# First edge stage of a two-layer graph network: the running sum of messages closed by a TensorE matmul and copied out by ScalarE

## What is computed

```
q_i = q[dst]; k_j = k[src]; v_j = v[src]
dk = silu(edge_attr @ Wdk.T + bdk); dv = silu(edge_attr @ Wdv.T + bdv)
attn = sum(q_i * k_j * dk, axis=1)
attn = silu(attn) * cosine_cutoff(edge_weight)
msg  = v_j * dv * attn[:, None]
agg  = segment_sum(msg, dst, num_segments=6250)
```

## Time and profile before

| | us |
|---|---|
| median of 3 runs | 3669.13 (3664.78 to 3677.05) |
| profiled execution | 3659.42 |
| its span, first to last instruction | 3657.6 |
| chunk loop of `edges_0` in it, first to last addition of a total | 265.4 to 1374.1 |

### The profile page before, as it was taken

How to read it: one execution, slowest core, us unless ns; L and a number is a source line. 1 busy time by engine, 2 the same in 40 slices (tenths; PEclk the granted TensorE clock), 3 DMA queues, 4 the chain that set the end, 5 groups by cost and what they waited for, 6 DMA issues and landing times. The chain is left out here.

```text
span 3657.6 us, 111781 instructions
## 1 busy us (share of the span) xinstructions
PE 3381.2 (92%) x25829; PEld 2771.8 (76%) x25830; DVE 3185.6 (87%) x9898; ACT 2594.7 (71%) x7607; POOL 2390.0 (65%) x2549
## 2 busy tenths in 40 slices
PE   3979999999999997996999999999999999997997
PEld 2547777777777775775888888888888888886996
DVE  6768999999999995664999999999999999996775
ACT  1856777777777774543878888888888888884553
POOL 3756777777777763554666666666666666663775
PEclk8989999999999997998999999999999999998998
DMA  3979999999999984776888888888888888884663
GB/s 102 263 230 309 301 296 301 298 298 298 299 298 300 300 253 165 276 258 224 254 235 239 240 236 239 237 239 237 238 238 239 238 237 239 236 237 150 213 208 126
DMA packets 604966, 898.40 MB, mean 246 GB/s; under 512 B 208971, under 2 KB 418646, under 8 KB 604371
## 3 DMA queue, kind: packets, MB, share of 16 engines
q0 software_dynamic: 164240, 566.71, 50.5%
q1 hardware_dynamic: 440643, 330.78, 30.2%
HBM read 724.25 MB, written 175.28 MB: 246 GB/s over the span
## 5 line engine op out<-in xcount | busy, mean ns | idle before, releaser
L1595 POOL DMA_INDIRECT kv1c<-kv_table,rec x900 | 865.9, 962 | 299.0 <-issue 284.6
L916 POOL DMA_INDIRECT kv<-kv_table,rec x832 | 848.3, 1020 | 282.3 <-issue 258.2
L1700 DVE CUSTOM_DVE_ANT_0 masked_scores<-score_p,far 126x384 f32<-126x384 f32 x1200 | 595.6, 551 | 30.2 <-issue 14.1
L1640 ACT ACTIVATE wv<-kv1c,wv 128x64 f32<-128x64 f32 x2400 | 605.9, 335 | 17.7
L954 ACT ACTIVATE gates<-gates_p 128x512 f32<-128x512 f32 x832 | 448.3, 591 | 77.5 <-PE gates_p L1087 77.5
L1803 PE MATMUL sum_p<-wv,hot 128*126 128x260 f32 x1800 | 477.7, 402 | 1.4 <-ACT wv L1640 1.4
L1759 PE MATMUL qe_p<-qrel,hotT 126*128 126x256 f32 x1800 | 443.0, 382 | 22.7 <-ACT hotT L1625 18.1
L1107 PE MATMUL sum_p<-msg,hot_weighted 128*124 128x256 f32 x1664 | 416.2, 393 | 5.3 <-ACT hot_weighted L962 5.3
L1759 PEld LDWEIGHTS qe_p<-qrel,hotT 126*128 126x128 f32 x1800 | 343.7, 191 | 74.9 <-ACT hotT L1625 18.7
L1107 PEld LDWEIGHTS sum_p<-msg,hot_weighted 128*124 128x124 f32 x1664 | 295.2, 187 | 116.2 <-issue 73.9
L1803 PEld LDWEIGHTS sum_p<-wv,hot 128*126 128x126 f32 x1800 | 316.1, 189 | 76.1 <-ACT wv L1640 1.8
(11 more groups left out here) (285 smaller groups left out, 7392.0 us busy)
## 6 DMA issues: line engine op xcount, KB each, us to landing
key<-segment_keys SPq DMA_DIRECT2D x300, 192.0 KB
q_blk<-q_table SPq DMA_DIRECT2D x208, 256.5 KB
acc_table<-acc SPq DMA_DIRECT2D x300, 130.0 KB
qrel<-q_by_relation SPq DMA_DIRECT2D x300, 128.0 KB
feat<-in_edge_feat_t SPq DMA_DIRECT2D x208, 128.0 KB
agg_and_x_plus_h<-total SPq DMA_DIRECT2D x208, 128.0 KB
kv1c<-kv_table,rec POOLq DMA_INDIRECT x900
kv<-kv_table,rec POOLq DMA_INDIRECT x832
```

The costliest lines, as they stand in the source:

```text
L916: pool.indirect_dma_start(kv[it.slot(AHEAD)][:, t, :], None, c["kv0_d"], bass.IndirectOffsetOnAxis(ap=rec[k][:, t, 0:1].bitcast(I32), axis ...
L1595: pool.indirect_dma_start(kv[k][:, t, :], None, c["kv1_d"], bass.IndirectOffsetOnAxis(ap=rec[k][:, t, 0:1].bitcast(I32), axis=0)).then_inc ...
L1640: ins = act.activation(wv[k][:, t, h, 0:DK], kv[s][:, t, D + h * DK:D + (h + 1) * DK], ACT.Copy, scale=wv[k][:, t, h, DK:DK + 1])
L1700: dve.tensor_tensor_reduce(junk[k][:, h], score_p[:, :, h, :], far[it.slot(U1)][:], 1.0, FLOOR, ALU.subtract, ALU.max, top[s][:, h:h + 1]) ...
```

## The change

DVE's `add_total` goes. In its place:

- ACT gets `same_diagonal(s-2)`: it scales a 124 x 124 identity by the flag `keep`, into one of two new buffers `same`.
- PE's `sum_messages(s-3)` gets a fifth 32-bit matmul into the same accumulation: `same` (124 x 124) against the total of the item before (124 x 256). Its four first matmuls now wait for the total of two items before instead of one, and the fifth waits for `same` and for the total of the item before.
- ACT gets `total_out(s-3)`: it copies the finished sum from PSUM into the slot of total. Both new functions stand ahead of `attn_silu` in ACT's order, `total_out` first.

```diff
--- before.py
+++ after.py
@@ -812,6 +812,7 @@
         weight = [sb(f"weight{k}", [P, T0]) for k in range(2)]
         msg = [sb(f"msg{k}", [P, T0, D]) for k in range(2)]
         total = [sb(f"total{k}", [P, D]) for k in range(U)]
+        same = [sb(f"same{k}", [GROUP, GROUP]) for k in range(2)]
         iota_0 = sb("iota_0", [P, GROUP])
         gates_p = [ps(f"gates_p{t}", [P, 2 * D]) for t in range(T0)]
         qe_p = ps("qe_p", [P, T0, D])
@@ -828,6 +829,7 @@
         qe_ready, qk_ready, attn_ready = sem("qe_ready"), sem("qk_ready"), sem("attn_ready")
         attn_act_ready, weight_ready = sem("attn_act_ready"), sem("weight_ready")
         msg_ready, msg_summed, total_ready = sem("msg_ready"), sem("msg_summed"), sem("total_ready")
+        same_ready = sem("same_block_diagonal")
         stored, held, iota_ready = sem("total_stored"), sem("edge0_held"), sem("iota_0_ready")
         LOADS = 3
 
@@ -954,6 +956,18 @@
                             act.activation(gates[k][:, t, :], gates_p[t][:], ACT.Silu).then_inc(gates_ready, 1)
                     return f
 
+                def total_out(it):
+                    k, s = it.slot(2), it.slot(U)
+                    wait(act, msg_summed, it)
+                    wait(act, stored, it, U, per=16)
+                    act.copy(total[s][0:GROUP], sum_p[:, k, :]).then_inc(total_ready, 1)
+
+                def same_diagonal(it):
+                    wait(act, keep_ready, it)
+                    wait(act, msg_summed, it, 2)
+                    act.activation(same[it.slot(2)][:], c["ident"][0:GROUP, 0:GROUP], ACT.Copy,
+                                   scale=keep[it.slot(U)][:]).then_inc(same_ready, 1)
+
                 def weigh_hot(it):
                     k = it.slot(2)
                     wait(act, weight_ready, it)
@@ -963,7 +977,7 @@
                                              scale=weight[k][:, t:t + 1])
                     ins.then_inc(hot_w_ready, 1)
 
-                run_chunks(act, steps, ((1, hot_out), (0, split_lead), (2, attn_silu), (1, gates_silu(1)),
+                run_chunks(act, steps, ((1, hot_out), (0, split_lead), (3, total_out), (2, same_diagonal), (2, attn_silu), (1, gates_silu(1)),
                                         (2, weigh_hot), (0, gates_silu(0))), U)
 
             @block.vector
@@ -1027,15 +1041,6 @@
                                                        ALU.mult, ALU.add, attn[k][:, t:t + 1])
                     ins.then_inc(attn_ready, 1)
 
-                def add_total(it):
-                    k, s = it.slot(2), it.slot(U)
-                    wait(dve, keep_ready, it)
-                    wait(dve, msg_summed, it)
-                    wait(dve, stored, it, U, per=16)
-                    wait(dve, total_ready, it, 1)
-                    dve.scalar_tensor_tensor(total[s][0:GROUP], total[it.prev().slot(U)][0:GROUP], keep[s][:],
-                                             sum_p[:, k, :], ALU.mult, ALU.add).then_inc(total_ready, 1)
-
                 def weights(it):
                     k, s = it.slot(2), it.slot(U)
                     wait(dve, attn_act_ready, it)
@@ -1054,7 +1059,7 @@
                                       ALU.mult).then_inc(msg_ready, 1)
 
                 run_chunks(dve, steps, ((2, q_times_k), (2, messages), (2, scores), (0, one_hot), (0, same_block),
-                                        (0, split_rest), (2, weights), (3, add_total)), U)
+                                        (0, split_rest), (2, weights)), U)
 
             @block.tensor
             def _(pe):
@@ -1102,11 +1107,13 @@
                     k = it.slot(2)
                     wait(pe, hot_w_ready, it)
                     wait(pe, msg_ready, it)
+                    wait(pe, total_ready, it, 2)
+                    for t in range(T0):
+                        pe.matmul(sum_p[:, k, :], hot_w[k][:, t, :], msg[k][:, t, :], start=t == 0, stop=False)
+                    wait(pe, same_ready, it)
                     wait(pe, total_ready, it, 1)
-                    for t in range(T0):
-                        ins = pe.matmul(sum_p[:, k, :], hot_w[k][:, t, :], msg[k][:, t, :],
-                                        start=t == 0, stop=t == T0 - 1)
-                    ins.then_inc(msg_summed, 1)
+                    pe.matmul(sum_p[:, k, :], same[k][:], total[it.prev().slot(U)][0:GROUP], start=False,
+                              stop=True).then_inc(msg_summed, 1)
 
                 run_chunks(pe, steps, ((1, edge_gates), (3, sum_messages), (1, q_of_edges), (0, turn)), U)
```

## The result

The changed kernel took 3721.8 us (median of 4 runs, 3716.8 to 3727.8), the one before 3667.0 beside it: ratio 1.0148, 95% interval 1.0135 to 1.0161, some 55 us slower. The forecast was slower by 90 us, 3759, with a range from 3738 to 3790. The sign was right, the size wrong, and the time lies outside the range: the change costs three fifths of what I had worked out.

A forecast was written before the change was run, and what follows sets the result against it. The prediction took the first edge stage to be PE-bound by its list; +86 us in the middle and +4 in ramp and drain, on 3669.1, gave 3759 us, range 3738 to 3790.

The forecast's parts named there:

- So PE's own list fills 5.27 of the 5.29 us: First edge stage: PE's gates, sums, q and transposes, summed start to start, take 5.27 us with no wait between.
- right behind: First edge stage: DVE and the loop through `qe_p`, 5.36 us in the step read, come just after PE's list.
- eight records in 1.99 us in the drain: Drain of first edge stage: sum records with data ready take the usual 1.99 us, so the pace is PE's own.
- The fifth matmul, 0.47 us: PE's message sums: two more records of 0.235 us each, making the step 5.74 us.
- the lower end of the range: Whole kernel: 3745 us with the ramp swallowed and runs near the profiled one; 3738 with some slack on PE.
- Rival 2: PE's list contains hidden slack that the fifth matmul fills; the `qe_p` loop keeps the pace, time 3669 us; chance 0.05.
- DVE's addition gives back nothing on the path: DVE loses 97.8 us of busy time, but `q_times_k` still waits for PE's q; 0.02 us a step taken.
- ACT's wait fits into the step: ACT's `total_out` waits for the same step's sum; its loop of 5.41 to 5.63 us stays under 5.74.
- DVE waits for ACT's silu, covered by q: DVE's `weights` waits for the later silu; DVE is back at about 807.1, PE's q ends at 807.18: barely covered.
- Other stages unmoved: Outside the first edge stage: all other stages run the same code, and everything behind the loop is merely shifted.
- PE still without idle time: Sign expected in the profile after: PE shows no idle time, in steps of 5.74 us.

The follow-up runs named there:

- e8: Changed kernel without its fifth matmul, ACT's copy and diagonal behind the gates, DVE's order q_times_k, one_hot, scores, messages: ratio 0.9906, step 5.131 us.
- e3: Kernel before, with DVE's addition cut to one of its 256 columns, nothing added to PE or ACT: ratio 0.9993, step 5.283 us.
- e10: Kernel before, with only DVE's order changed to q_times_k, one_hot, scores, messages: ratio 0.9987, step 5.276 us.
- e4: Kernel before, with DVE's addition cut to one column and DVE's scores put ahead of its messages: ratio 1.0001, step 5.319 us.
- e2: Kernel before, with two more 32-bit matmuls per step in the message sums (zero tile, adds nothing): ratio 1.0370, step 6.001 us.
- e1: Kernel before, with one more 32-bit matmul per step in the message sums (zero tile), DVE's addition kept: ratio 1.0146, step 5.571 us.
- e6: Changed kernel with ACT's copy and diagonal behind the gates and DVE's order q_times_k, one_hot, scores, messages: ratio 1.0130, step 5.570 us.
- e5: Changed kernel with ACT's copy and diagonal moved behind attn_silu and the second half of the gates, ahead of weigh_hot: ratio 1.0127, step 5.571 us.
- e12: Changed kernel with total and diagonal in rounded 32-bit format, ACT's copy behind the gates, DVE's order q_times_k, one_hot, scores, messages: ratio 0.9962, step 5.253 us.
- e11: Kernel before, DVE's order q_times_k, one_hot, scores, messages; ACT copies the sum from PSUM, DVE adds it from SBUF one step later: ratio 1.0041, step 5.396 us.

## Why the prediction was wrong

- **"So PE's own list fills 5.27 of the 5.29 us"**: this is the step that failed. The list takes 5.13 us (e8). I summed distances from start to start and took the lack of idle time between records for the lack of waiting. The record of the last sum reaches past the point where the next matmul could have begun, and q's late start lay under it. What held the step was the loop through `qe_p`: shorten DVE's list and nothing happens (e3), loosen the loop and PE's idle time ahead of q goes (e8, e10). The numbers for it stood in my own text: scores end at 805.39, q starts at 805.53, in a loop that I had summed to 5.36 us and called "right behind". It was in front.
- **The evidence that I gave for it**, eight records in 1.99 us in the drain, holds for the records of the sums among themselves, and says nothing of the wait between them and q. What I needed was q's start behind the sums with the scores done: 1.64 us (e4, e8), not 1.88.
- **The row that would have told**: the earlier trace rows counts 21 steps in which q's weight load waited for DVE. The rest of the idle time there, 44.6 us in 149 steps, was under "issue", and I left it out. The two together are 0.30 us a step over all 170 steps, of which 0.06 stay when nothing is waited for (e8).
- **The fifth matmul, 0.47 us**: mis-sized by a little. The full price is 0.43 to 0.44 (e2 less e1, e6 less e8); my 0.235 a record came from 1.88 / 8, which carried part of q's wait. For a part of it being hidden I had allowed next to nothing: 0.02 us a step in the forecast, 7 us in all at the lower end of the range (3745 to 3738), where the slack is 0.16 a step, 34 us. Rival 2 had the mechanism, hidden slack on PE, but counted only if the whole 0.47 was hidden, at a chance of 0.05. With the two terms right the sum is 208 x (5.131 + 0.44 - 5.295) = 57 us, and 63 with ACT's 0.03.
- **DVE's addition gives back nothing on the path**: right, and shown alone (e3). The reason holds too: `q_times_k` waits for q.
- **ACT's wait fits into the step**: right as to size. I had 5.41 to 5.63 us for its loop; it is 5.57, but beside a PE list of the same length and not of 5.74, which cost 0.03 us a step (e5).
- **DVE waits for ACT's silu, covered by q**: barely, as I said, and in part by luck. DVE waits 0.49 us ahead of `weights`, `q_times_k` starts at once behind it, at 808.44, and q ends at 807.11 + 1.28 = 808.39. Which of the two DVE would be idle for, I had the wrong way round.
- **Other stages unmoved**: right; the last total is 60.6 us later and so is the end.
- **"PE still without idle time"** was seen and proved nothing, before or after. The Trainium skill ("Perfetto Trace Analysis", Identifying the Most-Contended Engine) warns that matmul busy share is a poor measure of TensorE's headroom, and it was right here: busy 100%, slack 0.16 us a step, 3%. One of the two measures that it offers instead, the weight loads' busy share, was 78% before and 82% in e8, where PE's list alone is left. It pointed the right way without giving the size.

## What to carry to other kernels

An engine whose records leave no gap may still wait in every step. Take the start of each group that stands behind a semaphore, and ask whether it equals the end of what it waits for plus the usual hop (here 0.14 us). If it does, step after step, the engine's own list doesn't set the pace there, and new work on it is free as far as that wait reaches. How far that is takes a run: add the same work twice and see what the first and the second cost (here 0.28 and 0.43 us), or loosen the loop (0.16 us of slack). The idle time of the weight loads, "issue" included, can show such a wait where the matmuls' doesn't, but only beside a run without the wait: ahead of q it was 0.30 us a step against 0.06, ahead of the sums 0.53 with or without one, and 0.24 of difference were 0.16 of slack. Where two engines are full and a loop ties them, as here, moving work from one to the other costs its price on the receiver less that slack, and gains nothing on the giver.

## What the runs showed of the hardware

- A 32-bit matmul of 124x124 against 256 columns is two records and costs 0.43 to 0.44 us in a full stream at the 2.4 GHz level (granted clock 1.00; e2 less e1, e6 less e8); in the rounded format it is one record and costs about 0.12 (e12 less e8). With zeros as the stationary operand (e1) the step was the same as with the real diagonal (e5), 5.571.
- When the semaphore that q waits for is met early, its first record starts 0.03 us behind the start of the last sum's (e8: 804.09 + 1.99 - 0.38 = 805.70, q at 805.73) and the group lasts 1.14 us to the transposes; when it is met late, q starts 0.27 behind it (before: 803.65 + 1.99 - 0.38 = 805.26, q at 805.53) and lasts 1.02. So the distance from one group to the next moved by more than the slack, and only the distance over both groups, 2.90 against 2.76 to 2.78, gave its size.
- DVE's two-operand addition of 124x256 took 470 ns with one operand in PSUM (before) and 479 with all in SBUF (e11). The Trainium skill ("Perfetto Trace Analysis", Optimizing Scalar/DVE Operations) gives VectorE a smaller access overhead on SBUF than on PSUM, about 60 against 125 ns; this pair shows none of it.
